# ScalarE begins a layer's sums and cuts the rows at zero, in a graph network's layer change

## The chip, the core and the metric

The program runs on one core of a Trainium2 chip. The metric is the device time in microseconds (us) of one execution, lower is better; the time of a kernel is the median of its runs. The core's engines each work off their own queue in order: TensorE (PE, matrix products and turns), VectorE (DVE), ScalarE (ACT), GpSimd (POOL, which here issues the gathers), and SyncE (SP), which issues transfers. They wait for one another by semaphores.

## What is computed

A block of a graph transformer over 1250 nodes of 512 features and 40,000 edges sorted by target node. Four GINE layers stand in it, beside a linear attention and in front of a routed feed-forward with eight experts. The layers are what the change touches:

```python
def _gine_layer(x, src, dst, edge_attr, eps, We, be, W1, b1, gamma, beta, W2, b2):
    e = edge_attr @ We + be
    m = relu(x[src] + e)
    agg = segment_sum(m, dst, num_segments=x.shape[0])
    h = ((1.0 + eps) * x + agg) @ W1 + b1
    h = batch_norm(h) * gamma + beta
    h = relu(h)
    return relu(h @ W2 + b2)
```

All values are float32. The sum (1 + eps) * x + agg is kept turned (features on partitions, nodes along a row) in `aggT`, since it is the moving operand of the product with W1. So each layer begins by filling `aggT` with (1 + eps) * x, x being the last layer's result after its final ReLU.

## The kernel before

**A layer's messages.** The edges are cut into 53 chunks of 768. For an edge tile (128 edges), GpSimd gathers the source rows from the DRAM table `x_table` into `ring`, VectorE adds the edge's weight times We (L1108, the edge terms), ScalarE does the ReLU (L1712), and TensorE sums the tile into a window of 32 nodes by a one-hot product (L1931, the helper of nearly all matrix products). Windows are later turned and added to `aggT` (L1148). `ring` has four slots, so gathers of step j wait for TensorE's sums of step j - 4. In layers 1 to 3 (`MIXED`) a fourth of the chunks is not gathered: the source rows are picked by TensorE from `pieces`, the table split in three bf16 parts that stay in SBUF. A *take* (`take_rows`) is three bf16 products into bank ps4 or ps5, ScalarE cuts it at zero (L1752), and a *place* (`place_rows`) sums it with `pick_oh`, the picked places, which VectorE writes by comparisons (L1177).

**The passage between two layers.** The product with W2 runs in ten row tiles of 125 nodes. For each, VectorE adds the bias into `rowbuf` (L1477, `bias_row`), then writes ReLU + edge bias to a staging buffer (L1487, `stage_row`), from which SyncE stores the row to `x_table`. From the staged row ScalarE writes the high bf16 piece (L1758), VectorE the rest (L1497, `leave_rest`), ScalarE the mid piece (L1764), VectorE the last piece (L1503, `last_piece`). `rowbuf` itself stays without ReLU.

Then TensorE turns the ten rows of `rowbuf` (L2337, `columns_of`) into four banks in rotation, ps4, ps5, ps7 and ps1, and VectorE reads each bank and begins the sums with max(x, 0) times (1 + eps) (L1526):

```python
v.wait_ge(rowT, (l - 1) * NT + t + 1)
v.tensor_scalar(aggT[:, :, at:at + r], by_tile(turn_bank[t % 4][:, :])[:, :, 0:r], 0.0, eps1[:, bass.ds(l, 1)],
                ALU.max, ALU.mult).then_inc(agg_init if t < NT - 1 else flushed, 1)
```

`rowT` counts turned rows. `agg_init` counts begun sums, and turn t waits for t - 3 of them, when its bank is free. The tenth sum counts `flushed`, for which TensorE waits ahead of the layer's first take. `pick_oh` of chunk 0 lies over `rowbuf`, so it is written only when all rows are turned. The order on every engine is the order in which its code is written; nothing else plans it.

## Time and profile before

| | us |
|---|---|
| median of 3 runs | 1674.14 |
| lowest, highest | 1672.67, 1676.91 |
| the profiled execution | 1677.64 |
| its span in the trace | 1675.9 |
| TensorE, VectorE, ScalarE, GpSimd busy | 1443.3, 1201.6, 922.0, 1027.1 |
| mean granted clock of TensorE | 0.937 of full |

Times in the trace count from the span's start. The profiled execution's time is 1.7 us above its span. Busy times are totals over the whole span and do not tell which engine is late in a stage; for that one reads the chain of waits, and each engine's timeline in the stretch of interest. In a row of a timeline, a group "x4" begins at its first piece and its length runs to the end of the last; the bracket at the end is the time that the engine was idle before, and who ended it.

### The profile page before, as it was taken

Reading aid. Unit: us, or ns where it says so; the run is one execution under the profiler, and the core shown is the slowest. Engines: PE = TensorE matmul, PEld = TensorE weight load, DVE = VectorE, ACT = ScalarE, POOL = GpSimd, SP = SyncE. Lnnn points to the kernel's source line nnn. Section 1 sums busy time; section 2 is a strip of 40 time slices with the busy share of each in tenths; the row PEclk is TensorE's granted clock in tenths of the full one; section 3 lists DMA queues with packets and bytes.
Section 4 is the critical chain, followed back from the end, with each engine's and each line's share of the span. In section 5 each row is a group of like instructions: output and inputs, shape, how many; then the busy total and the mean of one; then the engine's idle time right before and its main releaser. Section 6 shows DMA issues by size and latency. Waiting matters only on the chain.

```text
span 1675.9 us, 21200 instructions
## 1 busy us (share of the span) xinstructions
PE 1443.3 (86%) x6734; PEld 603.8 (36%) x6734; DVE 1201.6 (72%) x2421; ACT 922.0 (55%) x1151; POOL 1027.1 (61%) x1070
## 2 busy tenths in 40 slices
PE   2787988879798988989889999897989989898597
PEld 2233333335443332323433333234423323244264
DVE  7688788986667777677486877675778777674644
ACT  3545454444445775767447767674467766573221
POOL 2777777777236777776066777772367777760133
PEclk9897999988998999999989999999999999898799
DMA  8666777787357777776377877784578777867443
GB/s 266 198 194 193 209 210 209 209 261 212 108 163 219 230 216 222 224 223 201 83 227 207 236 234 224 228 248 109 169 223 234 231 229 225 257 185 258 167 144 106
DMA packets 119091, 343.20 MB, mean 205 GB/s; under 512 B 20712, under 2 KB 24892, under 8 KB 118718
## 3 DMA queue, kind: packets, MB, share of 16 engines
q0 software_dynamic: 85248, 278.41, 56.9%
q1 hardware_dynamic: 32318, 60.78, 11.4%
q10 hardware_dynamic: 1408, 2.56, 0.5%
q8 instruction: 60, 0.98, 0.2%
q14 instruction: 57, 0.47, 0.1%
HBM read 323.61 MB, written 19.96 MB: 205 GB/s over the span
## 4 chain that ended last, share of the span: by engine, by line
PE 45%; DVE 18%; POOL 11%; issue 9%; DMA 8%; ACT 7%; DVEq 1%; POOLq 0%; SPq 0%; ACTq 0%
PE ps L1931 42%; POOL ring L897 11%; DVE ring L1108 10%; ACT ring L1712 6%; DMA ring<-x_table,idxT 5%; DVEq L1139 1%; DVE aggT L1526 1%; PE ps L2008 1%; DVE aggT L1148 1%; PE ps L2098 1%; DVE ring L1454 1%; DMA zT<-slot_table 1%; DMA ring<-in_x 1%; PE ps L2417 0%; DMA x_table<-ring 0%
## 5 line engine op out<-in xcount | busy, mean ns | idle before, releaser
L897 POOL DMA_INDIRECT ring<-x_table,idxT x1014 | 985.1, 972 | 478.5 <-issue 295.1
L1108 DVE SCALAR_TENSOR_TENSOR ring<-ps,wT,ring 128x512 f32<-128x512 f32 x930 | 626.9, 742 | 127.9 <-DMA ring<-x_table,idxT 122.8
L1712 ACT ACTIVATE ring<-ring 128x1536 f32<-128x1536 f32 x322 | 469.9, 1479 | 262.6 <-DVE ring L1108 261.8
L1931 PE MATMUL ps<-ring,onehot 128*32 128x512 f32 x2028 | 380.6, 642 | 131.9 <-ACT ring L1712 119.2
L1931 PE MATMUL ps<-zT,xT 128*32 128x512 f32 (+2 forms) x752 | 284.6, 604 | 0.0
L1931 PE MATMUL ps<-ring,zT 128*128 128x512 bf16 x1080 | 270.7, 381 | 2.2
L1752 ACT ACTIVATE zT<-ps 128x512 f32<-128x512 f32 x336 | 193.2, 595 | 134.5 <-PE ps L1931 130.3
L1931 PEld LDWEIGHTS ps<-ring,onehot 128*32 128x32 f32 x2028 | 60.1, 110 | 331.6 <-ACT ring L1712 274.9
L1931 PE MATMUL ps<-w,zT 128*125 128x512 f32 (+2 forms) x320 | 149.4, 631 | 15.1 <-ACT zT L1842 15.1
L1931 PEld LDWEIGHTS ps<-ring,zT 128*128 128x128 bf16 x1080 | 92.9, 98 | 185.5 <-ACT zT L1752 77.6
L1931 PE MATMUL ps<-aggT,w 128*128 128x256 f32 (+2 forms) x512 | 148.6, 439 | 6.0 <-DVE aggT L1148 6.0
L1931 PEld LDWEIGHTS ps<-aggT,w 128*128 128x128 f32 x512 | 98.2, 195 | 52.6 <-issue 35.2
L1931 PEld LDWEIGHTS ps<-zT,xT 128*32 128x32 f32 (+2 forms) x752 | 61.2, 119 | 112.0 <-issue 102.3
L1931 PEld LDWEIGHTS ps<-w,zT 128*125 128x125 f32 (+2 forms) x320 | 63.9, 201 | 98.7 <-issue 90.1
L1148 DVE TENSOR_TENSOR aggT<-ps,aggT 128x128 f32 x173 | 49.8, 288 | 31.5 <-PE ps L2008 15.4
L1108 DVE SCALAR_TENSOR_TENSOR ring<-we_bc,wT,ring 128x512 f32<-128x512 f32 x84 | 56.9, 746 | 18.8 <-DMA ring<-x_table,idxT 18.7
L1477 DVE TENSOR_TENSOR xT<-ps,stage 125x512 f32<-125x512 f32 (+2 forms) x40 | 27.7, 691 | 56.4 <-PE ps L1931 48.4
L1931 PE MATMUL ps<-ring,aggT 128*128 x204 | 65.8, 461 | 0.2 <-DVE aggT L1679 0.2
L963 POOL DMA_INDIRECT aggT<-pair_table,token_i x6 | 5.9, 989 | 86.7 <-DVEq L1644 85.2
L1931 PE MATMUL ps<-ring,xT 128*32 128x512 f32 x108 | 56.7, 607 | 0.0
L1162 DVE TENSOR_REDUCE lg<-ps 128x128 f32<-128x512 f32 x39 | 26.9, 691 | 34.4 <-PE ps L2098 19.8
L1752 ACT ACTIVATE ring<-ps 128x512 f32<-128x512 f32 x54 | 32.1, 595 | 21.6 <-PE ps L1931 21.1
(330 smaller groups left out, 1359.4 us busy)
## 6 DMA issues: line engine op xcount, KB each, us to landing
ring<-x_table,idxT POOLq DMA_INDIRECT x1014, 3.7
zT<-slot_table SPq DMA_DIRECT2D x36, 312.5 KB
w<-in_L_gnn_W SPq DMA_DIRECT2D x8, 1024.0 KB, 10.9
ring<-in_L_ffn_W SPq DMA_DIRECT2D x16, 512.0 KB, 9.6
x_table<-ring SPq DMA_DIRECT2D x24, 250.0 KB
x_table<-ring SPq DMA_DIRECT2D x9, 256.0 KB
stage<-in_x ACTq DMA_DIRECT2D x9, 256.0 KB
pair_table<-mix SPq DMA_DIRECT2D x9, 256.0 KB
```

Of the source, the lines that this page charges most:

```text
L897: gp.indirect_dma_start(out=to, out_offset=None, in_=table[:, :], in_offset=bass.IndirectOffsetOnAxis(ap=idx, axis=0)).then_inc(done, 16)
L1108: ins = v.scalar_tensor_tensor(out=at[:, x, :], in0=terms[:, :], scalar=wT[:, c, u:u + 1], in1=at[:, x, :], op0=ALU.mult, op1=ALU.add)
L1139: return v.value_load(base_i[0:1, c:c + 1], min_val=0, max_val=N - 1)
L1148: v.tensor_tensor(at, by_tile(ps[2])[:, :, i * WIN:(i + 1) * WIN], at, ALU.add).then_inc(flushed, 1)
L1162: step(v.tensor_reduce(group_sum, pick_fold[:, :].rearrange("p (a g n) -> p a n g", a=KD, g=G), AX.X, ALU.add))
L1454: v.tensor_scalar(marks[:, u, :], count[:, :], edge_of[:, 4, i * U + u:i * U + u + 1], None, ALU.is_equal).then_inc(marked, 1)
L1477: v.tensor_tensor(rowbuf[0:r, t, :], row_bank(t)[0:r, :], b2g_bc[0:r, :], ALU.add).then_inc(biased, 1)
L1526: v.tensor_scalar(aggT[:, :, at:at + r], by_tile(turn_bank[t % 4][:, :])[:, :, 0:r], 0.0, eps1[:, bass.ds(l, 1)], ALU.max, ALU.mult).then_ ...
L1712: a.activation(at, at, ACT.Relu).then_inc(relu_done, 1)
L1752: a.activation(picks[T % NH], take_bank(l, T)[:, :], ACT.Relu).then_inc(pick_relu, 1)
L1931: return nc.tensor.matmul(o, lhsT, rhs, start=start, stop=stop)
L2008: ins = pe.transpose(ps[2][:, m * P:m * P + q.stop], parts[q, (SB[l] + s) % 2, m * P:(m + 1) * P], ident[q, q])
```

## The change

ScalarE takes over two things of the passage. It cuts each row of `rowbuf` at zero in place (`cut_row`, behind the high piece), before TensorE turns it, so that TensorE's turns now wait for `row_cut` and not `biased`. And it begins the sums (`begin_sums`): an Identity with the scale (1 + eps), no ReLU being needed any more. VectorE keeps the pieces, and writes the first picked places behind the edge terms of step 1, with a wait for all ten turns and a new semaphore, `first_placed`, for TensorE's first place of the layer.

```diff
             def picked_places(q):
-                v.tensor_tensor(pick_oh[q % 2].rearrange("p a (s n) -> p a s n", n=WIN),
+                return v.tensor_tensor(pick_oh[q % 2].rearrange("p a (s n) -> p a s n", n=WIN),
...
                     for j in range(1, AHEAD_STEPS):
                         one_hots(l, j)
                         add_edges(l, j)
+                        if j == 1:
+                            v.wait_ge(rowT, l * NT)
+                            picked_places(0).then_inc(first_placed, 1)
...
-                for t in range(NT):
-                    at, r = row_tile(l - 1, t)
-                    v.wait_ge(rowT, (l - 1) * NT + t + 1)
-                    if t == NT - 1:
-                        picked_places(0)
-                    v.tensor_scalar(aggT[:, :, at:at + r], by_tile(turn_bank[t % 4][:, :])[:, :, 0:r], 0.0, eps1[:, bass.ds(l, 1)],
-                                    ALU.max, ALU.mult).then_inc(agg_init if t < NT - 1 else flushed, 1)
-                    if t == 1:
-                        last_piece(l, NT - 2)
-                    if t == 2:
-                        leave_rest(l, NT - 1)
-                    if t == 4:
-                        last_piece(l, NT - 1)
+                last_piece(l, NT - 2)
+                leave_rest(l, NT - 1)
+                last_piece(l, NT - 1)
...
+            def cut_row(l, t):
+                r = row_tile(l - 1, t)[1]
+                a.wait_ge(staged, (l - 1) * NT + t + 1)
+                a.activation(rowbuf[0:r, t, :], rowbuf[0:r, t, :], ACT.Relu).then_inc(row_cut, 1)
+
+            def begin_sums(l, t):
+                at, r = row_tile(l - 1, t)
+                a.wait_ge(rowT, (l - 1) * NT + t + 1)
+                a.activation(aggT[:, :, at:at + r], by_tile(turn_bank[t % 4][:, :])[:, :, 0:r], ACT.Identity,
+                             scale=eps1[:, l:l + 1]).then_inc(agg_init if t < NT - 1 else flushed, 1)
...
             def first_pieces(l):
                 high_piece(l, 0)
+                cut_row(l, 0)
                 for t in range(1, NT):
                     high_piece(l, t)
+                    cut_row(l, t)
                     mid_piece(l, t - 1)
                     if t == 1:
                         terms_copy(l)
-                mid_piece(l, NT - 1)
+                for t in range(NT):
+                    begin_sums(l, t)
+                    if t == 2:
+                        mid_piece(l, NT - 1)
...
             def place_rows(l, T):
+                if T == 0:
+                    pe.wait_ge(first_placed, MIXED.index(l) + 1)
...
             def columns_of(l):
-                    pe.wait_ge(biased, l * NT + max(t + 1, 8))
+                    pe.wait_ge(row_cut, l * NT + max(t + 1, 8))
```

VectorE's queue in the first passage, before, from the last row's staging to the edge terms of step 1 (L1503 last piece, L1497 rest, L1526 a begun sum, L1177 picked places, L1090 one-hots, L1108 edge terms):

```order
L1497 TENSOR_TENSOR ring<-ring 125x512 [waits pieces_ready,high_ready]
L1526 TENSOR_SCALAR aggT<-ps,eps 128x4x125 [waits rowT] x2
L1503 TENSOR_TENSOR ring<-ring 125x512 [waits mid_ready]
L1526 TENSOR_SCALAR aggT<-ps,eps 128x4x125 [waits rowT]
L1497 TENSOR_TENSOR ring<-ring 125x512 [waits pieces_ready,high_ready]
L1526 TENSOR_SCALAR aggT<-ps,eps 128x4x125 [waits rowT] x2
L1503 TENSOR_TENSOR ring<-ring 125x512 [waits mid_ready]
L1526 TENSOR_SCALAR aggT<-ps,eps 128x4x125 [waits rowT] x4
L1177 TENSOR_TENSOR xT<-iota,slot_rel 128x2x160 [waits rowT]
L1526 TENSOR_SCALAR aggT<-ps,eps 128x4x125
L1090 TENSOR_TENSOR onehot<-iota,relT 128x192 [waits parts_done,terms_ready]
L1108 SCALAR_TENSOR_TENSOR ring<-ps,wT,ring 128x512 [waits got0,dve_steps]
```

The same place of VectorE's queue now (L1508 last piece, L1502 rest, L1092 one-hots, L1110 edge terms, L1179 picked places):

```order
L1502 TENSOR_TENSOR ring<-ring 125x512 [waits pieces_ready,high_ready]
L1508 TENSOR_TENSOR ring<-ring 125x512 [waits mid_ready]
L1502 TENSOR_TENSOR ring<-ring 125x512 [waits pieces_ready,high_ready]
L1508 TENSOR_TENSOR ring<-ring 125x512 [waits mid_ready]
L1092 TENSOR_TENSOR onehot<-iota,relT 128x192 [waits parts_done,terms_ready]
L1110 SCALAR_TENSOR_TENSOR ring<-ps,wT,ring 128x512 [waits got0,dve_steps]
L1110 SCALAR_TENSOR_TENSOR ring<-ps,wT,ring 128x512 x5
L1179 TENSOR_TENSOR xT<-iota,slot_rel 128x2x160 [waits rowT]
L1092 TENSOR_TENSOR onehot<-iota,relT 128x192 [waits parts_done]
L1110 SCALAR_TENSOR_TENSOR ring<-ps,wT,ring 128x512 [waits got1,dve_steps]
```

The ten sums are gone from VectorE, its three last piece operations follow each other, and the picked places have moved behind the six edge terms.

ScalarE's queue at the same place, before (L1758 high piece, L1764 mid piece, L1752 ReLU of a take, L1712 ReLU of a step):

```order
L1758 ACTIVATE ring<-ring 125x512 [waits staged]
L1764 ACTIVATE ring<-ring 125x512 [waits rest_ready]
L1758 ACTIVATE ring<-ring 125x512 [waits staged]
L1764 ACTIVATE ring<-ring 125x512 [waits rest_ready] x2
L1752 ACTIVATE zT<-ps 128x512 [waits taken] x6
L1712 ACTIVATE ring<-ring 128x1536 [waits summed,windows_stored2]
```

And now (L1753 high piece, L1765 the row's ReLU, L1759 mid piece, L1771 a begun sum, L1747 ReLU of a take, L1707 ReLU of a step):

```order
L1753 ACTIVATE ring<-ring 125x512 [waits staged]
L1765 ACTIVATE xT<-xT 125x512 [waits staged]
L1759 ACTIVATE ring<-ring 125x512 [waits rest_ready]
L1771 ACTIVATE aggT<-ps,eps 128x4x125 [waits rowT] x3
L1759 ACTIVATE ring<-ring 125x512 [waits rest_ready]
L1771 ACTIVATE aggT<-ps,eps 128x4x125 [waits rowT] x7
L1747 ACTIVATE zT<-ps 128x512 [waits taken] x6
L1707 ACTIVATE ring<-ring 128x1536 [waits summed,windows_stored2]
```

Between the high piece and the mid piece stands the row's ReLU, and the ten sums stand between the last two mid pieces and the ReLUs of the takes.

## Rows read from the trace of the kernel before

**Rows 1.** The profile's page: engine totals; shares of the chain that ended last

```profile
PE 1443.3 (86%) x6734; PEld 603.8 (36%) x6734; DVE 1201.6 (72%) x2421; ACT 922.0 (55%) x1151; POOL 1027.1 (61%) x1070
...
PE 45%; DVE 18%; POOL 11%; issue 9%; DMA 8%; ACT 7%; DVEq 1%; POOLq 0%; SPq 0%; ACTq 0%
```

**Rows 2.** Chain that ended last, 478 to 540: start us, us, what ran

```profile
477.72 19.33 PE ps L1931 x45
...
498.52 0.64 ACT ring L1758
...
499.89 1.29 DVE aggT L1526 x2
...
508.61 5.63 PE ps L1931 x15
```

**Rows 3.** VectorE's timeline, first transition: start us, us, engine, line, what, idle before

```profile
499.20 0.69 DVE L1497 TENSOR_TENSOR ring<-ring 125x512 f32<-125x512 f32 x1
499.81 1.38 DVE L1526 TENSOR_SCALAR aggT<-ps,eps 128x500 f32<-128x500 f32 x2
...
504.84 2.67 DVE L1526 TENSOR_SCALAR aggT<-ps,eps 128x500 f32<-128x500 f32 x4
507.43 0.48 DVE L1177 TENSOR_TENSOR xT<-iota,slot_rel 128x320 f32<-128x320 f32 x1
507.83 0.73 DVE L1526 TENSOR_SCALAR aggT<-ps,eps 128x500 f32<-128x500 f32 x1
...
520.51 4.04 DVE L1108 SCALAR_TENSOR_TENSOR ring<-ps,wT,ring 128x512 f32<-128x512 f32 x6 [1.21 <-DMA ring<-x_table,idxT]
530.62 0.69 DVE L1162 TENSOR_REDUCE lg<-ps 128x128 f32<-128x512 f32 x1 [6.06 <-PE ps L2098]
```

**Rows 4.** ScalarE's timeline, the same stretch

```profile
498.52 0.63 ACT L1758 ACTIVATE ring<-ring 125x512 bf16<-125x512 f32 x1 [1.40 <-DVE ring L1487]
499.93 0.63 ACT L1764 ACTIVATE ring<-ring 125x512 bf16<-125x512 f32 x1 [0.77 <-DVE ring L1497]
...
515.65 2.85 ACT L1712 ACTIVATE ring<-ring 128x1536 f32<-128x1536 f32 x2
```

**Rows 5.** TensorE's timeline (matmuls), the same stretch

```profile
496.87 1.87 PE L2337 MATMUL ps<-ident,xT 125*128 125x125 f32 x16
...
503.82 2.96 PE L2337 MATMUL ps<-ident,xT 125*128 125x125 f32 x12 [0.48 <-DVE aggT L1526]
508.61 6.50 PE L1931 MATMUL ps<-ring,first_list 128*128 128x512 bf16 x18 [1.83 <-DVE aggT L1526]
515.04 1.06 PE L1931 MATMUL ps<-zT,xT 128*32 128x512 f32 x6
```

**Rows 6.** The groups by line and shape: count, busy us, mean ns, idle before

```profile
L1712 ACT ACTIVATE ring<-ring 128x1536 f32<-128x1536 f32 x322 | 469.9, 1479 | 262.6 <-DVE ring L1108 261.8
...
L1752 ACT ACTIVATE zT<-ps 128x512 f32<-128x512 f32 x336 | 193.2, 595 | 134.5 <-PE ps L1931 130.3
...
L1842 ACT ACTIVATE zT<-xT,sc 128x512 f32<-128x512 f32 x16 | 11.7, 799 | 0.0
...
L1842 ACT ACTIVATE zT<-ps,sc 128x226 f32<-128x226 f32 x16 | 7.2, 527 | 0.0
...
L1712 ACT ACTIVATE stage<-stage 128x512 f32<-128x512 f32 x4 | 2.5, 622 | 8.4 <-DVE stage L1108 8.4
```

**Rows 7.** ScalarE's timeline ahead of the rows, 456 to 470

```profile
465.73 1.80 ACT L1842 ACTIVATE zT<-ps,sc 128x226 f32<-128x226 f32 x4
```

**Rows 8.** Busy time by window (core 0: us, each engine), PEclk, DMA

```profile
502.00:504.00 2.00, 0.94 (x5) 0.62 (x6) 2.00 (x4) 0.63 (x1) 1.54 (x2) 0.73 0.89 282
...
512.00:514.00 2.00, 2.00 (x8) 0.71 (x6) 1.97 (x5) 0.96 (x2) 1.68 (x2) 0.71 0.96 263
```

**Rows 9.** TensorE's first takes in the third transition

```profile
1218.90 5.96 PE L1931 MATMUL ps<-ring,first_list 128*128 128x512 bf16 x18 [2.14 <-DVE aggT L1526]
```

**Rows 10.** GpSimd's timeline, the first gather of step 5

```profile
520.41 0.94 POOL L897 DMA_INDIRECT ring<-x_table,idxT  x1 [2.68 <-PE ps L1931]
```

2 lines of the change are left out of this document (added).

## The prediction

> **What bounds the kernel now.** Read the page first: TensorE is busy 86% of the span, VectorE 72%, ScalarE 55%, and the chain that ended last runs 45% through TensorE, 18% through VectorE, 7% through ScalarE [rows 1]. These are averages over stages with different limits, and the change touches only one stage: the passage from one layer to the next, which happens three times (from about 497, 852 and 1207 us). So what matters is whether VectorE's pieces there lie on the chain. The chain of waits says yes [rows 2]: the rows' matrix products end at 497.05, the last row goes through VectorE and ScalarE's first copy (498.52), and from 499.20 the chain stays on VectorE without a break until TensorE's first take at 508.61.
>
> The timelines show what that stretch of 8.7 us holds. VectorE begins the ten sums from 499.81 on, has two piece subtractions and one more in between, makes the first picked places at 507.43, and ends the last sum at 507.83 + 0.73 = 508.56 [rows 3]. TensorE turns four rows without waiting (496.87), then waits for the banks, and starts to take 0.05 us after the last sum [rows 5]. ScalarE is nearly empty: a copy at 498.52, one at 499.93 after 0.77 us of idling, and nothing but one more copy until TensorE's takes feed it [rows 4]. The takes wait because they use the banks that the turned rows lie in.
>
> **The change part by part.** The other two passages show the same pieces in the same order; I work out the first one and take it three times.
>
> *Removed from VectorE:* ten sums of 0.73 us. Four in a row take 2.67 us, so one follows another after (2.67 - 0.73) / 3 = 0.65 us [rows 3]. Ten of them 6.5 us, and the 0.48 us of picked places leaves the path as well.
>
> *Added to ScalarE, the ReLU of a row in place.* Ten a passage, 125x512, from SBUF to SBUF. The nearest row is the in-place ReLU of 512 columns, 622 ns [rows 6]. It stands between the high copy and the mid copy of each row, just where ScalarE idles 0.77 us for VectorE [rows 4]. So it costs nothing in the loop: 498.52 + 0.63 + 0.62 = 499.8, and the mid copy could not start before 499.93 anyway. Without that cover it would push the mid copy by 0.6 us. TensorE's turns now wait for these ReLUs, with eight rows cut before the first turn; a row's eight matrix pieces take 8 x 19.33 / 45 = 3.4 us [rows 2], so the eighth row was staged two rows, 6.9 us, ahead of the tenth (498.5) and is cut long before 496.87, and the last row's ReLU (499.8) is needed only for the tenth turn, after 505.
>
> *Added to ScalarE, the ten sums.* No row shows this form: 500 columns out of PSUM, scaled by a column of SBUF. From below: the plain ReLU out of PSUM takes 595 ns for 512 columns; from above: scale and bias from SBUF take 799 ns for 512 columns out of SBUF [rows 6]. The nearest row is scale and bias out of PSUM, 527 ns for 226 columns [rows 6]. A column costs (1479 - 622) / 1024 = 0.84 ns [rows 6], so 274 more make it 527 + 230 = 757 ns. Four of those pieces take 1.80 us together [rows 7], one every (1.80 - 0.53) / 3 = 0.42 us, so neighbours overlap by 0.10 us and I take 0.65 us from one sum to the next, the same as on VectorE.
>
> *The sum.* ScalarE ends the ninth row's mid copy at 499.93 + 0.63 = 500.56, then does three sums, the tenth row's mid copy (its subtraction on VectorE is over by 502.1: last piece from 500.6, rest from 501.4, 0.69 each), and seven sums. The last sum starts at 500.56 + 9 x 0.65 + 0.63 = 507.04 and ends at 507.8. Now TensorE: the fourth sum ends at 503.9 and frees the bank of the eighth turn; turns eight to ten take 2.96 us together [rows 5], to 507.0. So the banks and ScalarE come out equal, and the takes start at 507.85 in place of 508.61: **0.75 us earlier**. What shortens it is not a cheaper instruction but that two subtractions, a rest and the picked places no longer lie between the sums.
>
> The first takes run at half of TensorE's clock: the granted clock falls from 1.0 to 0.5 (2.4 to 1.2 GHz) within 502 to 504 and rises again within 512 to 514 [rows 8]. If the rise stays where it is, work begun 0.75 us earlier at half level is worth only half, 0.37 us; if it moves along, the whole. How much the clock's turn matters is seen in the third passage, where the same 18 takes last 5.96 us in place of 6.50 [rows 9, 5]. I take the middle, 0.55 us a passage.
>
> *Moved on VectorE:* picked places now stands behind the six edge terms of step 1, with a wait for the last turn (over at 507.0), and TensorE waits for it before its first place. VectorE is free at about 503.9, ends step 1 at about 504.3 + 4.0 = 508.3 and the places at 508.8. Before, TensorE's first place ran at 515.04 [rows 5]; 6 us of margin hide this wait. Queued behind VectorE's wait are only step 2's terms. No DMA and no queue entry of SP or GpSimd moves.
>
> *What VectorE gains.* It comes to step 1 some 4.6 us sooner (503.9 for 508.5). That brings nothing: ScalarE's ReLU of step 1 starts at 515.65, behind the take ReLUs in its queue [rows 4], when the terms have long been ready; step 3 has to wait for its gathers, which land at 520.5, and at 530.62 VectorE has idled 6.06 us for TensorE [rows 3]. Next late after the takes is the pair TensorE and ScalarE itself; GpSimd's gathers of step 5 wait 2.68 us for TensorE's sums of step 1 [rows 10], so they shift along and the gain goes on into the layer.
>
> Total: 3 x 0.55 = 1.6 us, of 1677.64 for the profiled execution (span 1675.9), giving 1676.0; the median of the runs is 3.5 us lower, 1674.14, and so the forecast is 1672.5. That is 0.1%; a measurement of this kernel can tell about 0.3% (5.0 us) from no change.
>
> **A rule against the change.** The trace has VectorE's sum at 0.73 us [rows 3] and my estimate for ScalarE's is 0.76. The Trainium skill ("ScalarE: Activation LUTs", section "Rules for kernel authors") advises to put relu, max and mul on VectorE and not ScalarE. These rows disagree with it for this case, since here both engines would be about equally long. Its section "What ACT_TABLE_LOAD costs" gives 186 ns + 0.833 ns a column, 93 ns more for each operand from SBUF, and 93 ns of overlap. By that, as an estimate, a sum takes 0.70 to 0.79 us and follows after 0.60 to 0.70, and a passage would gain 0.25 to 0.75 us.
>
> **The rivals.**
>
> *ScalarE's sums do not overlap, and it is slower than before.* Each sum waits for a turn, and if the engine drains at such a wait, one follows another after 0.76 + 0.04 = 0.80 us: the last ends at 500.56 + 9 x 0.80 + 0.67 + 0.76 = 509.2, 0.6 us late, at the price from above 0.9. For it: the copies of 498.52 and 499.93 never show overlap across a wait. Against: VectorE's sums wait for the same turns and overlap. It decides from 0.74 us a sum on. Three passages at half to whole worth: +1.5 us, 1675.6.
>
> *ScalarE's sums are cheap.* At the bound from below (0.585 for 500 columns, one every 0.49) the fourth sum ends at 503.25, the turns hold the rest to 506.35, and the takes start at 507.0: 1.6 us a passage, 2.4 to 4.8 in all, 1670.5 in the middle.
>
> *TensorE's clock comes back later.* The last turns end nearer to the takes but the order of pauses is another. If half level lasted over the takes and places from 513 to 515.04 + 1.06 = 516.1 as well [rows 5], those 3.1 us would take as long again: 9.3 us in three passages, 1683.4. It decides once the rise comes more than 1.7 us later than now. Against: the pause before the takes gets shorter.
>
> *The gain is absorbed further on,* for instance by the transfers of a layer: 1674.1. Against: GpSimd waits for TensorE at step 5 [rows 10].
>
> **How the numbers follow.** Forecast (0.37 to 0.75 us a passage; 1671.5 to 1673.2) 0.58; absorbed 0.12; cheap sums 0.12; no overlap 0.13; later clock 0.05. The three runs of before lie 4.2 us apart, so a median of the forecast's case may stand a microsecond or two off. The range 1669.5 to 1676.8 takes in the cheap and the dear sums. Faster by over 0.3% (below 1669.1) needs cheap sums at their full worth and a kind clock: 0.07. Slower by over 0.3% (above 1679.2) needs the clock: 0.06. Within: 0.87.
>
> **What would show it.** The sums on ScalarE at 0.75 us, 0.65 apart; the row ReLU inside the 0.77 us gap, so that the mid copies keep their beat of 3.4 us; the first take 7.9 us after the ninth row's mid copy starts (8.7 before); VectorE's idle ahead of step 3 and of the first fold grown by some 4 us; no TensorE wait for the picked places. Wrong would be: sums 0.8 apart, TensorE waiting for a row's ReLU, or a first take at the same place.

## The result

| | before | after |
|---|---|---|
| median, us | 1674.19 (5 runs) | 1666.48 (5 runs) |
| lowest, highest | 1672.67, 1676.94 | 1662.34, 1669.31 |
| the profiled execution; its span | 1677.64; 1675.9 | 1669.31; 1667.6 |
| mean granted clock of TensorE | 0.937 | 0.943 |

The ratio is 0.9945, with a 95% interval of 0.9929 to 0.9961. The changed kernel is faster by 9.2 us by that ratio (6.5 to 11.9), or by 7.7 us between the two medians. The forecast was a gain of 1.6 us and a range that ends at 1669.5, so the time lies 3.0 us outside it. The direction was right; the size was too small by a factor of five to six (1.6 against 7.7 or 9.2).

The page of the kernel after, the lines that answer to [rows 1]: busy time of each engine, and the shares of the chain that ended last.

```profile
PE 1427.5 (86%) x6662; PEld 600.8 (36%) x6734; DVE 1183.6 (71%) x2391; ACT 955.8 (57%) x1211; POOL 1027.5 (62%) x1070
...
PE 43%; POOL 16%; DVE 14%; issue 11%; DMA 8%; ACT 7%; DVEq 1%; POOLq 0%; SPq 0%; ACTq 0%
```

VectorE has 30 instructions and 18.0 us of busy time less, ScalarE 60 instructions and 33.8 us more. TensorE's 15.8 us less are not to be read as a gain: 72 of its 6734 products have no record in this trace. The chain has moved from VectorE (18% to 14%) to GpSimd (11% to 16%), and TensorE's share fell from 45% to 43%.

ScalarE's timeline in the first passage, for [rows 4] (start us, us, engine, line, what, idle before in brackets; L1753 high piece, L1765 the row's ReLU, L1759 mid piece, L1771 a begun sum, L1707 the ReLU of step 1):

```profile
500.92 0.63 ACT L1753 ACTIVATE ring<-ring 125x512 bf16<-125x512 f32 x1 [1.41 <-DVE ring L1492]
501.45 0.61 ACT L1765 ACTIVATE xT<-xT 125x512 f32<-125x512 f32 x1
502.32 0.63 ACT L1759 ACTIVATE ring<-ring 125x512 bf16<-125x512 f32 x1 [0.25 <-DVE ring L1502]
502.85 1.80 ACT L1771 ACTIVATE aggT<-ps,eps 128x500 f32<-128x500 f32 x3
504.54 0.63 ACT L1759 ACTIVATE ring<-ring 125x512 bf16<-125x512 f32 x1
505.05 4.09 ACT L1771 ACTIVATE aggT<-ps,eps 128x500 f32<-128x500 f32 x7
...
514.23 2.85 ACT L1707 ACTIVATE ring<-ring 128x1536 f32<-128x1536 f32 x2
```

The row's ReLU stands in the gap as forecast: it ends at 502.06, the mid piece starts at 502.32 and has still idled 0.25 us for VectorE. The ten sums run from 502.85 to 509.14 with one mid piece between them. Seven take 4.09 us, so one follows another after (4.09 - 0.73) / 6 = 0.56 us; I had forecast 0.65.

TensorE's matmuls there, for [rows 5] (L2352 turns, L1944 the helper; the trace lacks the record of the first of 18 take products, so "x17" begins about 0.25 us late):

```profile
499.27 1.87 PE L2352 MATMUL ps<-ident,xT 125*128 125x125 f32 x16
503.66 4.43 PE L2352 MATMUL ps<-ident,xT 125*128 125x125 f32 x24 [2.52 <-ACT aggT L1771]
509.43 4.26 PE L1944 MATMUL ps<-ring,first_list 128*128 128x512 bf16 x17 [1.33 <-ACT aggT L1771]
513.62 1.06 PE L1944 MATMUL ps<-zT,xT 128*32 128x512 f32 x6
```

And in windows, for [rows 8] (start:end, length, busy us of TensorE, then the granted clock, which is 1.00 at 2.4 GHz and 0.50 at 1.2 GHz):

```profile
502.00:504.00 2.00, 0.34 (x3) 1.00 0.81 282
504.00:506.00 2.00, 2.00 (x12) 0.50 0.68 184
506.00:508.00 2.00, 2.00 (x13) 0.65 0.70 223
508.00:510.00 2.00, 0.67 (x4) 1.00 0.82 206
...
512.00:514.00 2.00, 1.96 (x10) 1.00 0.79 166
```

These two views hold what the forecast missed. In the kernel before, the takes began at half level and got the full clock back near their end (at about 513), so that they took 6.50 us [rows 5, 8]. Now the pause ahead of turns 5 to 10 is one pause of 2.52 us, the 24 products behind it are one block that begins at half level, the clock is back at about 507, and the takes run at full level from their first product: 17 in 4.26 us.

That is the first passage only. In the second (and the third is like it) the 24 products come in two pieces, and the takes still begin at half level:

```profile
857.27 1.75 PE L2352 MATMUL ps<-ident,xT 125*128 125x125 f32 x12 [2.52 <-ACT aggT L1771]
859.49 2.73 PE L2352 MATMUL ps<-ident,xT 125*128 125x125 f32 x12 [0.47 <-ACT aggT L1771]
863.39 5.36 PE L1944 MATMUL ps<-ring,first_list 128*128 128x512 bf16 x17 [1.17 <-ACT aggT L1771]
```

The granted clock, read in windows of half a us with the share of a window split between the two levels, is at half level in these stretches (us after the passage's first turn):

| | first | second | third |
|---|---|---|---|
| before | 6.0 to 16.3 | 6.1 to 16.3 | 5.8 to 9.1, and 12.6 to 16.0 |
| after | 4.7 to 8.1 | 6.1 to 12.9 | 6.2 to 13.0 |

So the full clock is back sooner in all three, but ahead of the takes only in the first.

VectorE's timeline, for [rows 3] (L1110 edge terms of steps 1 and 3, L1179 picked places, L1164 the first fold, a reduction of four windows' sums):

```profile
506.19 4.04 DVE L1110 SCALAR_TENSOR_TENSOR ring<-ps,wT,ring 128x512 f32<-128x512 f32 x6
510.15 0.48 DVE L1179 TENSOR_TENSOR xT<-iota,slot_rel 128x320 f32<-128x320 f32 x1
...
523.47 4.04 DVE L1110 SCALAR_TENSOR_TENSOR ring<-ps,wT,ring 128x512 f32<-128x512 f32 x6 [5.36 <-DMA ring<-x_table,idxT]
529.19 0.69 DVE L1164 TENSOR_REDUCE lg<-ps 128x128 f32<-128x512 f32 x1 [1.68 <-PE ps L2113]
```

VectorE is at step 1 at 506.19, and idles 5.36 us ahead of step 3. The picked places are written at 510.63, 3.0 us before TensorE's first place at 513.62; TensorE does not wait for them.

The three passages side by side. To be independent of when a passage starts, times count from its first turn (496.87, 851.81, 1207.16 before; 499.27, 852.88, 1204.37 after). Starts of the takes are the end of the last sum plus 0.05 us where the trace lacks their first record.

| us after the first turn | before | after |
|---|---|---|
| last sum ends | 11.69, 11.74, 11.68 | 9.87, 10.06, 10.07 |
| takes start | 11.74, 11.80, 11.74 | 9.92, 10.11, 10.12 |
| ReLU of step 1 starts (L1712, L1707) | 18.78, 18.83, 18.23 | 14.96, 16.41, 16.42 |
| first fold (L1162, L1164) | 33.75, 33.80, 33.20 | 29.92, 31.38, 31.39 |

The sums end 5.1 us sooner over the three passages, and the stretch from the takes' start to the ReLU shrinks by another 2.9 us. That makes 8.1 us at the folds. From the ReLU of step 1 to the fold it is 14.97 us in all six columns. I call the time of the first fold after the first turn a passage's length from here on.

Does the layer keep it? GpSimd tells (start us, us, engine, line, what, idle before). First the kernel before, then the kernel after, each with the gather of step 5 that [rows 10] is about or its counterpart, and the first gather behind GpSimd's next long idling, the twelfth after that one:

```profile
541.59 0.94 POOL L897 DMA_INDIRECT ring<-x_table,idxT  x1 [5.67 <-issue]
```

```profile
521.78 0.95 POOL L899 DMA_INDIRECT ring<-x_table,idxT  x1 [0.30 <-issue]
...
540.16 0.94 POOL L899 DMA_INDIRECT ring<-x_table,idxT  x1 [3.56 <-issue]
```

Step 5's first gather waited 2.68 us for TensorE at 520.41 [rows 10]. Now it starts at 521.78 with only the 0.30 us that stand between any two gathers. The later one starts 541.59 - 496.87 = 44.72 us after the first turn before and 540.16 - 499.27 = 40.89 after: 3.83 us sooner, exactly what the first fold gained. Beyond that the layer runs at the pace at which GpSimd issues gathers, 0.95 + 0.30 = 1.25 us each, so what is gained by here is handed on: the layer's last gather starts 293.7 us after the first turn in the nine layers of three traces of the kernel before, and 290.9 in the six layers of two traces of the kernel after. That is 2.8 us sooner a layer, as much as the passages are shorter on average.

At the layer's end it gets unsteady. The layers, counted from one first turn to the next, take 354.94 and 355.35 us before, 353.61 and 351.49 after. The first is 1.3 us shorter where its passage gained 3.8, the second 3.9 where its passage gained 2.4. In the first, the 32 products that begin the layer's dense part start 3.0 us sooner (+304.45 for +307.48) but take 8.06 us in place of 6.37.

### The profile page after: what moved, and what is told of

Read it like the earlier page. It is cut to its first block, busy times and chain, and to the rows that moved or that the text cites. A ratio compares the mean times of both kernels' runs of the same rounds, so it can differ in the third digit from the quotient of the medians.

```text
span 1667.6 us, 21159 instructions
## 1 busy us (share of the span) xinstructions
PE 1427.5 (86%) x6662; PEld 600.8 (36%) x6734; DVE 1183.6 (71%) x2391; ACT 955.8 (57%) x1211; POOL 1027.5 (62%) x1070
## 4 chain that ended last, share of the span: by engine, by line
PE 43%; POOL 16%; DVE 14%; issue 11%; DMA 8%; ACT 7%; DVEq 1%; POOLq 0%; SPq 0%; ACTq 0%
PE ps L1944 40%; POOL ring L899 15%; DVE ring L1110 8%; DMA ring<-x_table,idxT 6%; ACT ring L1707 5%; DVEq L1141 1%; ACT aggT L1771 1%; PE ps L2021 1%; DVE aggT L1150 1%; DMA ring<-in_x 1%; DMA zT<-slot_table 1%; PE ps L2113 1%; PE ps L2432 0%; DVE ring L1459 0%; DVE ring L1023 0%
## 5 line engine op out<-in xcount | busy, mean ns | idle before, releaser
L1110 DVE SCALAR_TENSOR_TENSOR ring<-ps,wT,ring 128x512 f32<-128x512 f32 x930 | 626.9, 742 | 143.8 <-DMA ring<-x_table,idxT 139.3
L1707 ACT ACTIVATE ring<-ring 128x1536 f32<-128x1536 f32 x322 | 470.7, 1480 | 265.5 <-DVE ring L1110 264.7
L1944 PE MATMUL ps<-ring,onehot 128*32 128x512 f32 x2028 | 378.0, 638 | 133.4 <-ACT ring L1707 121.1
L1944 PE MATMUL ps<-zT,xT 128*32 128x512 f32 (+2 forms) x752 | 285.8, 605 | 0.0
L1944 PE MATMUL ps<-ring,zT 128*128 128x512 bf16 x1014 | 260.2, 382 | 9.2 <-issue 4.0
L1747 ACT ACTIVATE zT<-ps 128x512 f32<-128x512 f32 x336 | 193.2, 595 | 114.6 <-PE ps L1944 106.4
L1944 PEld LDWEIGHTS ps<-ring,onehot 128*32 128x32 f32 x2028 | 59.2, 110 | 336.6 <-ACT ring L1707 277.8
L1944 PE MATMUL ps<-w,zT 128*125 128x512 f32 (+2 forms) x320 | 147.1, 623 | 15.1 <-ACT zT L1855 15.1
L1944 PEld LDWEIGHTS ps<-ring,zT 128*128 128x128 bf16 x1080 | 93.0, 98 | 185.4 <-ACT zT L1747 77.4
L1944 PE MATMUL ps<-aggT,w 128*128 128x256 f32 (+2 forms) x512 | 150.3, 443 | 6.0 <-DVE aggT L1150 6.0
L1944 PEld LDWEIGHTS ps<-aggT,w 128*128 128x128 f32 x512 | 99.4, 198 | 53.0 <-issue 35.4
L1944 PEld LDWEIGHTS ps<-zT,xT 128*32 128x32 f32 (+2 forms) x752 | 60.3, 118 | 109.5 <-issue 102.0
L1944 PEld LDWEIGHTS ps<-w,zT 128*125 128x125 f32 (+2 forms) x320 | 63.0, 198 | 97.3 <-issue 89.9
L1110 DVE SCALAR_TENSOR_TENSOR ring<-we_bc,wT,ring 128x512 f32<-128x512 f32 x84 | 56.9, 745 | 17.4 <-DMA ring<-x_table,idxT 17.3
L1944 PE MATMUL ps<-ring,aggT 128*128 x204 | 65.4, 459 | 0.2 <-DVE aggT L1674 0.2
L1944 PE MATMUL ps<-ring,xT 128*32 128x512 f32 x108 | 55.8, 599 | 0.0
L1164 DVE TENSOR_REDUCE lg<-ps 128x128 f32<-128x512 f32 x39 | 26.9, 690 | 27.7 <-DVE aggT L1150 14.9
L1747 ACT ACTIVATE ring<-ps 128x512 f32<-128x512 f32 x54 | 32.1, 595 | 21.3 <-PE ps L1944 20.8
```

The lines of the kernel that those rows point to most:

```text
L1110: ins = v.scalar_tensor_tensor(out=at[:, x, :], in0=terms[:, :], scalar=wT[:, c, u:u + 1], in1=at[:, x, :], op0=ALU.mult, op1=ALU.add)
L1164: step(v.tensor_reduce(group_sum, pick_fold[:, :].rearrange("p (a g n) -> p a n g", a=KD, g=G), AX.X, ALU.add))
L1707: a.activation(at, at, ACT.Relu).then_inc(relu_done, 1)
L1747: a.activation(picks[T % NH], take_bank(l, T)[:, :], ACT.Relu).then_inc(pick_relu, 1)
L1944: return nc.tensor.matmul(o, lhsT, rhs, start=start, stop=stop)
```

## The experiments

The theory after the result: **the gain is the sum of the three passages' shortening, made of an earlier last sum and an earlier return of TensorE's clock.** Rivals are that the gain comes from VectorE's head start, from the pace of the engine that begins the sums, from the picked places' move, or from one mechanism (the clock) alone. Each run is put beside one account: the lengths of its three passages in the trace, against 100.5 us for the kernel before (nine passages of three traces). The ratio is taken to runs of the kernel before on the same chip, and a difference in us is (ratio - 1) x 1675. The passages are the steady part of a trace: outside of them the seventeen traces hold between 1569.1 and 1580.1 us, so that a single trace says nothing of a few us in the whole, and only the ratio of many runs does.

### The same sums, paced as slowly as before

The kernel after, with three idle operations of ScalarE ahead of sums 1, 4 and 9, so that the last sum ends when it did before. VectorE is as free as after.

```diff
                 for t in range(NT):
+                    if t in (1, 4, NT - 1):
+                        a.wait_ge(idled, MIXED.index(l) * 3 + (1, 4, NT - 1).index(t))
+                        a.activation(ps[0][:, 0:4 * SR], we_bc[:, 0:4 * SR], ACT.Identity, scale=eps1[:, l:l + 1]).then_inc(idled, 1)
                     begin_sums(l, t)
```

> The changed kernel with three more ScalarE operations of about 0.7 us between the sums (ahead of the second, the fifth and the tenth), so that the tenth sum ends some 11.7 us after the first turn begins, as before the change; VectorE keeps its earlier start on step 1. Theory 1 (pace: the gain comes from when TensorE's turns and takes run, and from the level of its clock meanwhile): first takes at +11.7 us with a length of 6.0 to 6.5 us, all of the gain gone, 1673 to 1676. Theory 2 (VectorE's lead on the steps carries part of the gain): takes at +11.7 but half or more of the gain stays, 1668 to 1670. Theory 3 (the clock follows from the ten sums and not from the pause): takes at +11.7 but only 4.3 to 5.4 us long, 1670 to 1672.

Measured 1667.89 (12 runs), ratio 0.9960 (0.9942 to 0.9977). TensorE's matmuls in its first passage:

```profile
496.25 1.87 PE L2356 MATMUL ps<-ident,xT 125*128 125x125 f32 x16
500.65 0.62 PE L2356 MATMUL ps<-ident,xT 125*128 125x125 f32 x4 [2.52 <-ACT aggT L1772]
501.81 4.40 PE L2356 MATMUL ps<-ident,xT 125*128 125x125 f32 x20 [0.55 <-ACT aggT L1772]
508.21 4.26 PE L1948 MATMUL ps<-ring,first_list 128*128 128x512 bf16 x17 [2.00 <-ACT aggT L1772]
```

The last sum ends at +11.67, as before, and yet the takes run at full level in two of three passages (the third took 5.73 us). Passages 31.72, 31.72 and 33.22, which makes -3.8 us; measured -6.7 (-9.7 to -3.9). Its turns 5 to 10 are nearly one block, and so a part of the trace's gain does not need an earlier last sum: it is TensorE's clock. How large that part is, this run does not settle. The measured gain is 2.9 us above the account, at the edge of its interval, and the time (1667.89) lies where the second theory, VectorE's lead, had put it; what speaks against that theory is only the run with VectorE held back, below. Between these two kernels, measured on the same chip, the account has 5.3 us and the ratios 2.5. For this I have no cause.

### Only the clock, without the change

The kernel before, with 16 idle turns behind the fourth row's turn and 8 behind the tenth, so that TensorE is busy in its pauses.

```diff
                     ins.then_inc(rowT, 1)
+                    for c in range({3: 16, NT - 1: 8}.get(t, 0)):
+                        pe.transpose(ps[0][:, c % KD * P:(c % KD + 1) * P], ident[:, :], ident[:, :])
```

> The kernel before with idle turns on TensorE in its pauses: 16 behind the fourth turn, 8 behind the tenth, of the identity matrix into a bank that nobody reads. VectorE's sums end where they did. Theory 1 (the clock's level in the passage is worth as much as the earlier start): the granted clock stays at 1.0 or comes back before the takes, their 6.5 us become 4.3 to 5.4, 1.1 to 2.2 us a passage, 1668 to 1671. Rival (the takes are long for another reason, for instance ScalarE's ReLUs between them): takes stay 6.0 to 6.5 us, 1674.

Measured 1674.53 (12 runs), ratio 0.9989 (0.9973 to 1.0005). The windows of this kernel are at 1.00 throughout the passage, and its takes take 4.26 us:

```profile
502.00:504.00 2.00, 1.34 (x10) 1.00 0.85 268
504.00:506.00 2.00, 1.37 (x13) 1.00 0.76 243
506.00:508.00 2.00, 0.54 (x5) 1.00 0.72 185
508.00:510.00 2.00, 1.79 (x8) 1.00 0.37 114
```

Passages 31.74, 31.73, 31.73, so 5.3 us shorter by the account, of which 1.8 were measured (-4.5 to +0.8). The takes did what the first theory said, the time what its rival said. The account says too much here, by 3.5 us.

### Only the picked places moved

The kernel before with the picked places behind step 1, and nothing else of the change.

```diff
+                        if j == 1:
+                            v.wait_ge(rowT, l * NT)
+                            picked_places(0).then_inc(first_placed, 1)
...
-                    if t == NT - 1:
-                        picked_places(0)
```

> The kernel before, only with the first picked places moved behind step 1 on VectorE and TensorE's wait for them. All sums stay on VectorE. Expected: the tenth sum ends 0.44 us earlier in each passage (+11.25 us after the first turn), takes at +11.3, 1672.5 to 1674 by the pieces alone. If the clock comes back earlier in the takes as well, up to 1670. If TensorE has to wait for the places, which VectorE now writes after step 1 at about +16.8 us against a first place at +18.1, slower than before: 1675 or more.

Measured 1671.97 (12 runs), ratio 0.9979 (0.9963 to 0.9996). The last sum ends at +11.29, 0.4 us sooner. Passages 32.90, 32.83 and 31.39: -3.4 us, measured -3.5. Again more than the 3 x 0.4 us of the sum alone. The rest is that the pause before the takes shrinks (1.4 us for 1.8 in the first) and the takes are over sooner (5.66, 5.59 and 4.26 us for the 17 of them on record).

### VectorE gets nothing of its head start

The kernel after; VectorE writes the picked places, then waits for the tenth sum, and only then makes the edge terms of step 1.

```diff
                 if l in MIXED:
+                    v.wait_ge(rowT, l * NT)
+                    picked_places(0).then_inc(first_placed, 1)
+                    v.wait_ge(flushed, l * (NC + 1) + 3)
                     for j in range(1, AHEAD_STEPS):
```

> The changed kernel, but VectorE writes the picked places and then waits for the tenth sum before it starts on step 1, so that it has no lead over the kernel before. Theory 1 (pace and clock on TensorE): same time as the changed kernel, 1665 to 1668, step 1's ReLU on ScalarE still at +15.0 to +16.4 us. Theory 2 (VectorE's lead): 1670 to 1674. A small loss is possible under both, since VectorE would end step 1 at about +14.5 us, close to where ScalarE wants it.

Measured 1667.40 (8 runs), ratio 0.9945 (0.9927 to 0.9964), the same ratio as the change itself. VectorE's edge terms of its first passage, at +10.30 where the kernel after has them at +6.92:

```profile
507.33 0.49 DVE L1179 TENSOR_TENSOR xT<-iota,slot_rel 128x320 f32<-128x320 f32 x1 [2.30 <-PE ps L2352]
...
508.71 4.04 DVE L1110 SCALAR_TENSOR_TENSOR ring<-ps,wT,ring 128x512 f32<-128x512 f32 x6
```

Passages 29.92, 30.09, 31.39 (-9.1; measured -9.2). VectorE's head start of some 3.4 us has no worth that these runs can show. Its interval (-12.2 to -6.0 us) would hide three us either way, but the trace of the first passage has no place for them, since the ReLU of step 1 starts at +14.95, as after.

### The kernel before, twice more

The kernel before again, once each, to know how far its passages differ from one execution to the next.

> The kernel before, unchanged, for a second trace of its three passages. If the stretch at half clock in the takes is a fixed property of the passage, the 18 takes last 6.0 to 6.5 us again in all three and the fold comes at +33.2 to +33.8 us. If the clock's turns fall differently from execution to execution, some of them are 4.3 to 5.7 us long, and the average gain of a steady clock is smaller than the first trace of before lets it seem.

> The same once more: a third trace of the kernel before. Same expectations as the second.

1678.16 and 1678.80 in one execution each. Passages are 33.12, 33.73, 33.79 and 33.20, 33.84, 33.15. So a passage of the kernel before is either about 33.15 or about 33.8 us long, and never near 29.9 or 31.4. The account is good to about a microsecond.

### The change with TensorE kept busy

The kernel after with 20 idle turns behind the fourth and 8 behind the tenth.

```diff
+                    for c in range({3: 20, NT - 1: 8}.get(t, 0)):
+                        pe.transpose(ps[0][:, c % KD * P:(c % KD + 1) * P], ident[:, :], ident[:, :])
```

> The changed kernel with idle turns on TensorE: 20 behind the fourth turn, 8 behind the tenth. If the clock level matters on average, takes 4.26 us in all three passages, and the turns at full level, fold at +29.3 to +29.9 us: 1 to 3 us faster than the changed kernel, 1663 to 1666. If a steady clock is given back later (as the kernel before with idle turns gained nothing clear), equal to the changed kernel, 1666 to 1668.

Measured 1665.85 (12 runs), ratio 0.9945 (0.9926 to 0.9965). Passages 29.93, 29.92, 29.94 (-10.7; measured -9.2). The idle turns pull passages 2 and 3 to the length of the first, and bring the kernel nothing that can be told from noise. The changed kernel already has nearly all that the clock can give in this stretch.

### Sums split between the engines

The kernel after, but VectorE begins the sums of the first two rows.

```diff
+                for t in range(2):
+                    at, r = row_tile(l - 1, t)
+                    v.wait_ge(rowT, (l - 1) * NT + t + 1)
+                    v.tensor_scalar(aggT[:, :, at:at + r], by_tile(turn_bank[t % 4][:, :])[:, :, 0:r], eps1[:, bass.ds(l, 1)], None,
+                                    ALU.mult).then_inc(first_sums, 1)
...
-                for t in range(NT):
+                for t in range(2, NT):
                     begin_sums(l, t)
-                    if t == 2:
+                    if t == 5:
                         mid_piece(l, NT - 1)
```

> The changed kernel, but VectorE, which waits for ScalarE's mid copy there, begins the sums of the first two rows; ScalarE begins the other eight. Expected by the passage's account: the fifth turn can start some 1.0 us earlier (+3.4 for +4.4 us after the first), the tenth sum ends 0.5 to 1.0 us earlier, takes at +9.3 to +9.8, 1.5 to 3 us in all: 1664 to 1666. If TensorE's turns at half clock are the bound, no gain.

Measured 1665.58 (11 runs), ratio 0.9938 (0.9917 to 0.9959). TensorE's matmuls:

```profile
501.13 1.87 PE L2361 MATMUL ps<-ident,xT 125*128 125x125 f32 x16
504.95 2.97 PE L2361 MATMUL ps<-ident,xT 125*128 125x125 f32 x24 [1.94 <-DVE aggT L1530]
510.15 5.74 PE L1950 MATMUL ps<-ring,first_list 128*128 128x512 bf16 x17 [2.24 <-ACT aggT L1777]
```

The last sum ends at +8.75, 1.1 us sooner than after. The 24 turn products now lie at full level (2.97 us for 4.43), but 2.24 us of pause follow, and from 510 to 514 the granted clock is 0.57 on average: 17 takes need 5.74 us for 4.26. Passages 30.26, 30.31, 30.25 (-9.7; measured -10.4). The 1.1 us are given back in the takes of every passage; against the kernel after, only its passages 2 and 3 were longer, and a difference of 1 us is not clear of noise.

### Without the row's ReLU, and with it alone

The kernel after without `cut_row`; the sums are Relu with the scale.

```diff
-                a.activation(aggT[:, :, at:at + r], by_tile(turn_bank[t % 4][:, :])[:, :, 0:r], ACT.Identity,
+                a.activation(aggT[:, :, at:at + r], by_tile(turn_bank[t % 4][:, :])[:, :, 0:r], ACT.Relu,
                              scale=eps1[:, l:l + 1]).then_inc(agg_init if t < NT - 1 else flushed, 1)
...
-                cut_row(l, 0)
...
-                    pe.wait_ge(row_cut, l * NT + max(t + 1, 8))
+                    pe.wait_ge(biased, l * NT + max(t + 1, 8))
```

> The changed kernel without the in-place ReLU of the rows; ScalarE's sums do a ReLU with the scale instead (the product is cut after the scale, so for layers with a negative factor the result is another). Theory 1 (the passage decides): same passage as the changed kernel (fold at +29.9 to +31.4), same time, 1665 to 1668. If the cut of the rows costs something hidden, faster by more than 1 us.

Measured 1666.64 (6 runs), ratio 0.9940 (0.9919 to 0.9961). Passages 29.93, 30.10, 29.93 (-10.5; measured -10.1).

And the kernel before with `cut_row` alone, TensorE's turns waiting for it:

```diff
                 high_piece(l, 0)
+                cut_row(l, 0)
...
-                    pe.wait_ge(biased, l * NT + max(t + 1, 8))
+                    pe.wait_ge(row_cut, l * NT + max(t + 1, 8))
```

> The kernel before with only the in-place ReLU of the rows added on ScalarE, and TensorE's turns waiting for it. VectorE begins the sums as before. Expected: passage as before (takes at +11.7 to +12.1, fold +33.1 to +33.8), 1674 to 1676. If the ReLU in place has a worth of its own, faster; if it disturbs the pieces, slower than 1677.

Measured 1675.77 (12 runs), ratio 1.0000 (0.9985 to 1.0015). Passages 33.72, 33.79, 33.73 (+0.7; measured 0). The row's ReLU costs nothing, and brings nothing by itself. What it allows, the plain scale on ScalarE, is no better than Relu with the scale.

### Picked places moved, and TensorE kept busy

The third experiment and the second together, on the kernel before.

> The kernel before with the picked places moved and with the idle turns: both changes of the passage that need no work on ScalarE. By the passage's account: takes at +11.5, 4.26 us long, fold at +31.3 in all three, 2.2 us a passage, 1668 to 1670. If the gain of idle turns is given back further on, as their single run let it seem (expected 1668 to 1671, measured 1674.5), 1671 to 1674.

Measured 1672.21 (12 runs), ratio 0.9959 (0.9941 to 0.9978). Takes at +11.34, 4.49 us for all 18, passages 31.33 three times (-6.5; measured -6.9).

### The change once more

> The changed kernel again, for a second trace and for more runs on the same chip as the others of this set: 1664 to 1668; fold at +29.9 to +31.4 in each passage, so that the part of the clock can be told from one passage to another.

Measured 1666.91 (6 runs), ratio 0.9935 (0.9913 to 0.9958). TensorE's matmuls, in a trace with all 18 records:

```profile
501.65 4.41 PE L2352 MATMUL ps<-ident,xT 125*128 125x125 f32 x24 [2.52 <-ACT aggT L1771]
507.18 4.49 PE L1944 MATMUL ps<-ring,first_list 128*128 128x512 bf16 x18 [1.12 <-ACT aggT L1771]
```

The takes start at 507.18 - 497.25 = +9.93 and take 4.49 us. Passages 29.93, 31.38, 30.11 (-9.1; measured -10.9).

### ScalarE's sum with a bias column

The sum's price in the forecast came from a row whose operation has both a scale and a bias from SBUF. This kernel is the one after, with a column of zeros as the bias.

```diff
                 a.activation(aggT[:, :, at:at + r], by_tile(turn_bank[t % 4][:, :])[:, :, 0:r], ACT.Identity,
-                             scale=eps1[:, l:l + 1]).then_inc(agg_init if t < NT - 1 else flushed, 1)
+                             bias=nil[:, 0:1], scale=eps1[:, l:l + 1]).then_inc(agg_init if t < NT - 1 else flushed, 1)
```

> The changed kernel, its sums with a bias taken from a column of zeros as well as the scale. The forecast took a sum's length from a row with scale and bias. If the second column is what that row pays for, a sum takes 0.75 us here, one every 0.65, in place of 0.69 and 0.57, and the tenth sum ends at +10.6 in place of +9.9 to +10.1 us: the forecast's step was right for another instruction. If the lengths stay at 0.69, the error was in the cost of a column or of the start.

1664.60 in one execution. The group of the sums (count, busy us, mean ns of one, idle before), of the kernel after and then of this one, and ScalarE's timeline of this one:

```profile
L1771 ACT ACTIVATE aggT<-ps,eps 128x500 f32<-128x500 f32 x30 | 17.9, 694 | 0.1
```

```profile
L1773 ACT ACTIVATE aggT<-ps,nil,eps 128x500 f32<-128x500 f32 x30 | 20.4, 782 | 0.0
```

```profile
498.96 2.07 ACT L1773 ACTIVATE aggT<-ps,nil,eps 128x500 f32<-128x500 f32 x3
...
501.44 4.72 ACT L1773 ACTIVATE aggT<-ps,nil,eps 128x500 f32<-128x500 f32 x7
```

782 ns in place of 694, and one every (4.72 - 0.79) / 6 = 0.65 us in place of 0.56. This is the forecast's sum (757 ns, one every 0.65 us) to within 4%. The takes begin at +10.84, that is 0.9 us before [rows 5] and 0.9 us behind the kernel after. The forecast said 507.85 - 496.87 = +10.98. So its working was sound for the instruction that it priced. Passages 30.84, 30.83, 30.82: -8.0 us by the account, although only 3 x 0.9 = 2.7 come from the sums' end. So in this one trace the clock makes the gain large even with the sums as dear as forecast.

### Keeping TensorE busy, again

The second experiment once more, since its measurement fell short of the account.

> The kernel before with idle turns once more, on another chip. Its passages are 1.8 us shorter each by its first trace (fold +31.7 for +33.5), so -5.3 us by the account of the passages; measured were -2.2 on the mean of 12 runs. If that was the spread of the runs, -4 to -6 us now; if idle turns give something back, -1 to -3 again.

Measured 1674.51 (12 runs), ratio 0.9986 (0.9969 to 1.0003). Passages 31.73, 31.73, 31.79 (-5.3; measured -2.3, from -5.2 to +0.5). The shortfall is there again, 3 us.

### Split sums with TensorE kept busy

The split kernel with 4 idle turns behind the fourth and 8 behind the tenth.

> The split of the sums between VectorE (rows 0 and 1) and ScalarE, with idle turns (4 behind the fourth turn, 8 behind the tenth). By the account of the passages: tenth sum at +8.4 to +8.8, takes 4.5 us long, fold at +28.5 to +29.0 in all three: 1.5 to 2.5 us faster than the changed kernel in all three passages taken one by one (some 4 to 6 us together), 13 us below the kernel before. If TensorE's turns or the clock take it back, as the split alone (-10.0 us on the mean).

Measured 1666.02 (6 runs), ratio 0.9936 (0.9912 to 0.9960). Takes at +8.80, 4.49 us, passages 28.79, 28.80, 28.80: -14.1 us by the account, the shortest of all, and yet -10.7 measured (-14.7 to -6.7). The trace shows a place where such a gain may be lost, the end of the layer. Windows of TensorE there, of this kernel and then of the first experiment's:

```profile
798.00:800.00 2.00, 1.41 (x4) 0.70 0.00 0
800.00:802.00 2.00, 2.00 (x7) 0.50 0.01 4
802.00:804.00 2.00, 2.00 (x11) 0.95 0.00 0
```

```profile
800.00:802.00 2.00, 0.66 (x4) 1.00 0.00 0
802.00:804.00 2.00, 2.00 (x13) 1.00 0.01 4
```

And the first matrix products of the layer's dense part in each (start us, us, then what):

```profile
798.59 8.06 PE L1950 MATMUL ps<-aggT,w 128*128 128x226 f32 x32 [1.34 <-DVE aggT L1151]
```

```profile
801.39 6.37 PE L1948 MATMUL ps<-aggT,w 128*128 128x226 f32 x32 [1.34 <-DVE aggT L1151]
```

The same 32 products take 8.06 us where the clock falls ahead of them and 6.37 where it does not: 1.7 us for one layer's end. Each trace has three such ends behind its three passages. The 32 products take 7.9 to 8.1 us in four of nine in the kernel before, in two of six in the kernel after, in all three here, in two of three with the picked places moved and TensorE filled, in one of three in the first experiment's and in each of the two traces of the kernel before filled, and in none of three in the filled change. It comes and goes at 1.7 us a layer, and I cannot show that it follows the passage. For the kernel before filled, where the account is 3 us too large, it is no more frequent than in the kernel before.

### All of it in one table

Passage lengths from the trace; account is their sum less 100.5; measured is (ratio - 1) x 1675.

| kernel | passages | account | measured (95%) |
|---|---|---|---|
| the change | 29.92, 31.38, 31.39 | -7.8 | -9.2 (-11.9 to -6.5) |
| the change again | 29.93, 31.38, 30.11 | -9.1 | -10.9 (-14.6 to -7.0) |
| VectorE late | 29.92, 30.09, 31.39 | -9.1 | -9.2 (-12.2 to -6.0) |
| no row ReLU | 29.93, 30.10, 29.93 | -10.5 | -10.1 (-13.6 to -6.5) |
| change, filled | 29.93, 29.92, 29.94 | -10.7 | -9.2 (-12.4 to -5.9) |
| split | 30.26, 30.31, 30.25 | -9.7 | -10.4 (-13.9 to -6.9) |
| split, filled | 28.79, 28.80, 28.80 | -14.1 | -10.7 (-14.7 to -6.7) |
| change, slow pace | 31.72, 31.72, 33.22 | -3.8 | -6.7 (-9.7 to -3.9) |
| before, filled | 31.74, 31.73, 31.73 | -5.3 | -1.8 (-4.5 to +0.8) |
| before, filled, again | 31.73, 31.73, 31.79 | -5.3 | -2.3 (-5.2 to +0.5) |
| places only | 32.90, 32.83, 31.39 | -3.4 | -3.5 (-6.2 to -0.7) |
| places, filled | 31.33, 31.33, 31.33 | -6.5 | -6.9 (-9.9 to -3.7) |
| row ReLU only | 33.72, 33.79, 33.73 | +0.7 | 0.0 (-2.5 to +2.5) |

Nine of thirteen agree within 2 us. The account lies outside the interval for the kernel before with TensorE filled, at the interval's edge for its repetition and for the slow pace, and inside for the other ten; but the interval is about 6 us wide, so this tests the whole of the passages' gain and hardly its two parts. No version beats the changed kernel by more than its interval.

## Why the prediction was wrong

**Right: the stage, the path and the carrying on.** The chain did lie on the ten sums; the takes start 0.05 us behind the last sum before and after; and an earlier first fold came out again as earlier gathers, 3.83 us for 3.83. The way was not the one named: step 5's first gather, which was to shift along, starts only 1.0 us sooner (+22.51 for +23.54) and waits for TensorE no longer; it is the gather twelve further on that moves by the whole. The rival that the gain is absorbed further on fell. So did the one that the sums do not overlap: they follow at 0.56 us. But in the first passage each turn was over before its sum could start (the last at +8.82, the tenth sum starts at about +9.2), so overlap across a true wait was not put to the test there. The first take came 6.9 us after the ninth mid piece's start, where 7.9 was forecast.

**Right: everything costed at nothing.** The row's ReLU sits in the gap (0.61 us in 0.77, 0.25 left), measured at 0 by itself. The mid pieces keep their beat, 3.43 us. The picked places are ready 3.0 us before they are needed. VectorE's head start shows no worth (VectorE held back: the same ratio). One sign of it came out otherwise: VectorE's idle time ahead of step 3 grew by 4 us as forecast (1.21 to 5.36), but ahead of the first fold it fell from 6.06 to 1.68, since the fold comes 3.8 us sooner and step 3's gathers land no sooner (its terms start at +24.20 for +23.64).

**Wrong, the smaller part: the price of a sum.** "The nearest row is scale and bias out of PSUM" gave 757 ns and one every 0.65 us. The operation here has no bias column. It took 694 ns, one every 0.56; with a bias column it takes 782 and 0.65. Over nine steps that is 9 x 0.09 = 0.8 us, with a shorter last sum and mid piece 1.0 us: the last sum ended 1.8 us earlier in the first passage and 1.6 to 1.7 in the others, where the takes were to start 0.75 earlier. In the other two ScalarE was not the bound, but TensorE's turns at half level, which ended at +9.34 and not at +8.82. The bound from below, "cheap sums", had this very gain of 1.6 us in the takes' start. It was kept as a rival with 0.12, and a time below 1669.1, which "needs cheap sums at their full worth and a kind clock", with 0.07. That is what came.

**Wrong, the larger part: the worth of the clock.** The step that failed is "if the rise stays where it is, work begun 0.75 us earlier at half level is worth only half; if it moves along, the whole", and with it 0.55 us a passage, the term of the sum that was mis-sized. Both ends of that took the clock for a discount on a gain, and left out that the change can bring the clock back sooner by more than the work moved. The pauses between the turns changed too: before, turns 5 to 10 came in three pieces with a pause each, and a last pause of 1.83 us stood ahead of the takes [rows 5]. In the first passage they are now one block, with a last pause of about 1.1 us. The clock came back 8.1 us after the first turn in place of 16.3, before the takes and not near their end, and the 18 takes need 4.5 us in place of 6.50. In the other two passages turns 5 to 10 are two pieces with a last pause of about 0.8 us, and the clock came back within the takes, at 12.9 and 13.0 for 16.3 and 16.0. From the takes' start to the ReLU of step 1 that makes 7.04 - 5.04 = 2.0 us in the first passage, and 0.7 and 0.2 in the others: 2.9 us of the 8.1. Why the clock falls at 4.7 in one passage and at 6.1 in another of the same kernel, no run shows. The third passage of the kernel before had the hint: the forecast took its shorter takes (5.96 us) for a small shift of one rise, but the clock was back there already at 9.1 and fell a second time at 12.6. In the kernel "places only" the same effect makes 0.4 us of earlier sums worth 1.1 us.

**How the terms add up.** Forecast 3 x 0.55 = 1.6, which is 3 x 0.75 = 2.25 from the takes' start less 0.6 for the clock. Trace: 1.8 + 1.7 + 1.6 = 5.1 from the sums' end and 2.9 more from the clock, 8.1 in all (the terms are rounded). So the term of the sums' end was short by 2.9 us and the term of the clock by 3.5. Measured 9.2, from 6.5 to 11.9. This split is read from the traces; by measured times alone it is uncertain, as the slowly paced change shows.

The Trainium skill's page "ScalarE: Activation LUTs", section "What ACT_TABLE_LOAD costs", had the sum nearer than the row did: 186 ns + 0.833 ns x 500 + 93 ns for the scale column, which is an operand by pointer, gives 696 ns, as an estimate, and the trace has 694. With the bias column as well 789 against 782. Its overlap of 93 ns is too small here, 694 - 560 = 134 ns. The advice in its section "Rules for kernel authors" to put relu and mul on VectorE, for which it gives speeds in bf16, does not hold for these operands: fp32 out of PSUM takes 0.73 us every 0.65 on VectorE [rows 3], and 0.69 every 0.56 on ScalarE.

**Open.** Why TensorE filled in the kernel before brings 2 us where the passages are 5.3 shorter, and why the slowly paced change brings more than its passages. Two sets of twelve executions agree on the first. Their two traces narrow down where it is lost: in their six layers the last gather starts 291.9 us after the first turn, 1.7 sooner than in the kernel before and as much as the passages are shorter, but the 32 products of the dense part start at 306.2 for 306.8, only 0.7 sooner (in the kernel after, 304.1: the whole 2.8). So a us a layer goes between the last gather and the dense part. Single layers scatter by 3 us at that place, 304.6 to 308.1, so this is an indication and no proof. The half-level stretch within the 32 products does not account for it, and no run was made that changes the layer's end alone.

## What to carry to other kernels

Price an operation on ScalarE by its operands, each column of scale or bias by itself, and not by the nearest row with one column more. Where a row of short waits stands in front of a matrix stage and the granted clock falls there, look at what the change does to the pauses of TensorE, and in every passage, not in the first alone: here its work moved together, the clock came back ahead of the next stage or earlier within it, and by the traces that made 3 of 8 us. And look for the engine that paces what follows (here GpSimd, 1.25 us a gather): it decides whether a gain at the start of a stage is kept.

## What the runs showed of the hardware

- ScalarE reading 128x500 fp32 out of PSUM with a scale column: 0.69 us, one every 0.56 us although each carries a wait on a semaphore, which was met by then; with a bias column also, 0.78 and 0.65. VectorE's same work is 0.73 and 0.65 [rows 3].
- Sixteen 125x125 fp32 turns take 1.87 us at full level; 24 of them take 2.97 at full level (the split kernel) and 4.43 where the level is half for most of the block (the kernel after).
- 18 bf16 products of 512 columns take 4.49 us at full level, and 5.76 to 6.54 when the clock changes within them.
- Idle turns in TensorE's pauses held the granted clock at 1.00 over all three passages, in all five runs that had them (four kernels). They made each passage of the kernel before 1.8 us shorter, 5.3 in all, but its time fell by 1.8 and 2.3 us only, and neither can be told from no change by itself.
